# Cross-attention and feed-forward block: VectorE's low halves of weights and turned tokens at the end of its feed-forward slot, the second x1 turning two slots after the first

## The chip, the cores and the metric

The kernel runs on one core of a Trainium2 chip. Its time is the device time of one execution in microseconds (us); the figure compared is the median of several. The engines are TensorE (PE: matmuls), VectorE (DVE), ScalarE (ACT), GpSimd (POOL) and SyncE (SP: here it issues nearly all DMAs).

## The reference

Sixteen batches of 512 tokens, model width 512, 16 heads of 32, feed-forward width 2048:

```python
q, k, v = heads(x @ Wq + bq), heads(ctx @ Wk + bk), heads(ctx @ Wv + bv)
scores = einsum('bhqd,bhkd->bhqk', q, k) / sqrt(32)
attn = softmax(where(j < i, scores, -1e30)); attn[:, :, 0, :] = 0
x1 = layer_norm(x + merge(attn @ v) @ Wo + bo) * g1 + be1
out = layer_norm(x1 + relu(x1 @ W1 + b1) @ W2 + b2) * g2 + be2
```

Everything is float32. The kernel writes each float32 operand as a high half (a rounded copy) and a low half (operand minus high half) and makes a product of three matmuls: high by high, high by low, low by high.

## The kernel before, in words

Two programs, `attention` and `feed`, are each written as five generators, one per engine, which yield once per slot. `side_by_side` runs the attention's slots alone for a while; from attention slot 768 + 38 on, each engine does one feed-forward slot after every two attention slots, and when the attention's 864 slots are over, the rest of the feed-forward slots follow. So the order of each engine's queue is fixed by hand, by slot numbers; engines meet only through semaphores.

The feed-forward program works on chunks of T = 256 tokens (two halves u = 0, 1 of 128), 32 chunks, each in windows of 16 slots. A step at slot number n of a chunk falls into slot n mod 16 of the window n / 16 later; `due(window, s, SLOTS, CHUNKS, first)` says for which chunk that is now. In one slot each engine goes through its steps in the order in which they are written. Three chunks overlap.

The steps of a chunk, with their slot numbers:

- LOAD (0): SyncE loads attention rows into `o_in` in 32-token blocks (8 DMAs, L847) and then x into `x_in` (L853). It waits until the previous chunk's x1 has been turned (`x1_turned`) and its residual taken. ADD_BO (2, 3): GpSimd adds the bias to `x_in` (L1096).
- OTR (turn at 2 and 4, halves at 3 and 5): VectorE transposes the blocks into `block_turned` (L1249), a single buffer; ScalarE copies the high half (L1143), VectorE subtracts to get the low half (L1264) in `turned`. A turn waits for the low half before it (`turned_lo`).
- PROJ (5, 6): TensorE multiplies by Wo into `front` (L1355); half u waits for `turned_lo`.
- RES (6, 7): VectorE adds `x_in` and takes statistics (L1286, L1190); NORM1 (8) normalises into `x1`. SyncE then stores x1 in DRAM (L1061, slot 9) and loads it back in blocks into the same `o_in` (slots 10 and 11).
- X1_TURN: VectorE turns the x1 blocks (L1249), ScalarE copies the high half (L1131), VectorE makes the low half (L1259) in `x1_halves`; GpSimd adds b2 to x1 (L1103).
- FFN1 (16 to 31): TensorE, 12 matmuls a slot into `h_ps` (L1369). The first waits for both x1 halves.
- ScalarE's relu into `hf` (L1183), GpSimd's three mixing additions (L1109 to L1112, every other slot), ScalarE's high half (L1172, odd slots) and VectorE's low half (L1329, even slots) in `hs`: the second product is made from 7 products of mixed blocks where 8 would be plain.
- FFN2 (22 to 37): TensorE, 12 or 9 matmuls a slot into `acc` (L1385).
- RES2 - 1 (37), which is slot 5: VectorE takes `acc` out in four operations (L1299 twice, L1304 twice) once 15 of the 16 FFN2 steps are done; RES2 (38): two more (L1312, L1315). STATS2 (42), NORM2 (46, slot 14): second normalisation, whose square root is ScalarE's (L1118) and whose last two operations are L1222. STORE (47, slot 15): SyncE stores `y` (L1080).
- In the first slots of the program the 48 weight pieces are split too, about 1.5 a slot in slots 5 to 33: SyncE loads, ScalarE takes the high half (L1157, L1159), VectorE the low half (L1273, L1276), and SyncE waits for the low half (`w_lo`) before it loads the next piece into the same buffer (L1076).

VectorE's steps of one slot are written in this order: turn, low half of the turned tokens, low halves of weights, RES, NORM1, RES2 - 1, RES2, STATS2, NORM2, low half of hs. The slots in which the turns and their halves stand come from one expression:

```python
for kind, at in ((0, OTR), (1, X1_TURN)):
    for u in range(U):
        for item, _ in due(window, s, SLOTS, CHUNKS, at + (1 + 2 * u, u)[kind]):
```

With kind 1 (x1) turn and halves of u are both in slot X1_TURN + u.

## Time and profile before

| | |
|---|---|
| median of 3 runs | 2663.69 us (2663.68 to 2664.45) |
| the profiled execution's own time | 2661.86 us |
| its span, first to last instruction | 2660.0 us |
| granted TensorE clock, mean | 0.987 |
| PE busy | 2596.9 us, 98% |
| VectorE busy | 2077.8 us, 78% |
| ScalarE busy | 1525.6 us, 57% |
| GpSimd busy | 1556.8 us, 59% |

Busy time is the time in which an engine executes; what is left of the span are waits. The granted clock is a share of TensorE's full speed; 1.00 is the 2.4 GHz level. In rows of the timeline the first number is the start from the span's first instruction, the second the duration, and a bracket at the end says how long the engine had been idle before and what released it. In profile rows `x` stands for x1 or x1's DRAM tensor, `x_halves` for `x1_halves`, `W` for W1 or W2.

### The profile page before, as it was taken

To read this page: it belongs to the slowest core of one execution; us is meant where nothing else is said; L and a number is where in the kernel's file an instruction comes from. 1 tells how busy PE (TensorE), PEld (TensorE's weight loads), DVE (VectorE), ACT (ScalarE), POOL (GpSimd) and SP (SyncE) were. 2 spreads that over 40 slices of the span, in tenths; PEclk is the share of its full clock that TensorE was granted. 3 is DMA by queue.
4 is the path that set the end of the run, shared out by engine and by line. 5 is a ranking of instruction groups with operands and counts; after the bars stand their busy time and mean duration, and the time that the engine had idled before them with its cause. 6 is when DMAs were issued, how large, how long until landed. Compare 5 with 4: busy or idle time off the path is not lost.

```text
span 2660.0 us, 62128 instructions
## 1 busy us (share of the span) xinstructions
PE 2596.9 (98%) x22540; PEld 2237.7 (84%) x22540; DVE 2077.8 (78%) x5171; ACT 1525.6 (57%) x2945; POOL 1556.8 (59%) x1721
## 2 busy tenths in 40 slices
PE   7999999999999999878999999999999999999998
PEld 5888888888888888757888888888888888888887
DVE  6889888988888888788767767676767676767675
ACT  4777787787777877677343434343434344444433
POOL 3777777766666666566555545454555544454543
PEclk9999999999999999978999999999999999999999
DMA  7666655565555655556132222222222222222220
GB/s 194 156 154 157 162 152 155 153 151 149 146 141 147 152 140 141 138 135 176 42 70 50 69 52 67 54 64 57 57 64 57 64 57 64 56 65 56 64 57 25
DMA packets 439556, 273.35 MB, mean 103 GB/s; under 512 B 299648, under 2 KB 334400, under 8 KB 439248
## 3 DMA queue, kind: packets, MB, share of 16 engines
q1 hardware_dynamic: 438288, 267.79, 40.4%
q8 instruction: 178, 2.92, 0.5%
q10 hardware_dynamic: 960, 1.57, 0.3%
q14 instruction: 130, 1.06, 0.1%
HBM read 109.86 MB, written 57.67 MB: 63 GB/s over the span
## 4 chain that ended last, share of the span: by engine, by line
PE 92%; DVE 3%; SPq 1%; issue 1%; DMA 1%; POOL 1%; ACT 1%; ACTq 0%; DVEq 0%; POOLq 0%
PE h_ps L1369 25%; PE acc L1385 22%; PE lin_ps L708 13%; PE front L1355 6%; PE lin_ps L704 6%; PE max_ps L683 6%; PE st_ps L730 6%; PE o_ps L750 4%; PE o_ps L752 3%; PE st_ps L765 2%; POOL prob_lo L429 1%; DVE W L1276 1%; SPq L847 0%; ACTq L492 0%; SPq L354 0%
## 5 line engine op out<-in xcount | busy, mean ns | idle before, releaser
L429 POOL TENSOR_TENSOR prob_lo<-probs,prob_hi 128x512 f16<-128x512 f32 (+1 forms) x768 | 784.4, 1035 | 371.7 <-ACT prob_hi L508 366.9
L1369 PE MATMUL h_ps<-x_halves,W 128*128 128x256 f16 x6144 | 756.4, 273 | 2.0 <-ACT hf L1183 2.0
L1385 PE MATMUL acc<-W,hs 128*128 128x256 f16 x5376 | 669.6, 273 | 1.0 <-DVE hs L1329 1.0
L1369 PEld LDWEIGHTS h_ps<-x_halves,W 128*128 128x128 f16 x6144 | 596.5, 98 | 87.8 <-issue 16.8
L1183 ACT ACTIVATE hf<-h_ps,b1s,scale_evac 128x256 f32<-128x256 f32 x512 | 284.8, 562 | 583.5 <-PE h_ps L1369 581.6
L664 DVE CUSTOM_DVE_ANT_0 max_ps<-max_ps,mask_q 128x128 f32<-128x128 f32 (+3 forms) x1024 | 485.5, 505 | 129.3 <-PE max_ps L683 113.2
L1385 PEld LDWEIGHTS acc<-W,hs 128*128 128x128 f16 x5376 | 525.9, 98 | 62.2 <-issue 1.5
L506 ACT ACTIVATE probs<-st_ps 128x512 f32<-128x512 f32 (+1 forms) x768 | 406.5, 529 | 244.2 <-PE st_ps L765 227.2
L1109 POOL TENSOR_TENSOR hf<-hf 128x256 f32<-128x256 f32 x256 | 237.7, 928 | 500.6 <-ACT hf L1183 500.4
L508 ACT ACTIVATE prob_hi<-st_ps 128x512 f16<-128x512 f32 (+1 forms) x768 | 406.8, 530 | 0.0
L1329 DVE TENSOR_TENSOR hs<-hf,hs 128x896 f16<-128x896 f32 x256 | 279.1, 1109 | 142.9 <-ACT hs L1172 142.9
L1172 ACT ACTIVATE hs<-hf 128x896 f16<-128x896 f32 x256 | 241.8, 945 | 239.4 <-POOL hf L1112 235.8
L730 PE MATMUL st_ps<-heads 98*128 98x512 f32 (+3 forms) x1024 | 313.5, 347 | 10.2 <-ACT prob_hi L508 5.3
L683 PE MATMUL max_ps<-heads 96*128 96x128 f32 (+3 forms) x1024 | 279.6, 325 | 11.9 <-DVE maxima L664 10.0
L750 PE MATMUL o_ps<-V,prob_hi 128*128 128x97 bf16 x2560 | 246.6, 209 | 10.9 <-DVE onorm L596 8.8
L752 PE MATMUL o_ps<-V,prob_lo 128*128 128x65 bf16 x2560 | 241.2, 194 | 0.0
L683 PEld LDWEIGHTS max_ps<-heads 96*128 96x128 f32 x1024 | 184.1, 191 | 61.1 <-DVE maxima L664 20.4
L704 PE MATMUL lin_ps<-wv,ctxT 128*128 128x512 f32 x768 | 226.1, 405 | 7.2 <-DVE ctxT L521 7.2
L708 PE MATMUL lin_ps<-xT,wq 128*128 128x512 f32 x768 | 226.1, 403 | 3.9 <-DVE vf L630 3.0
L1110 POOL TENSOR_TENSOR hf<-hf 128x256 f32<-128x256 f32 x256 | 224.3, 876 | 0.0
L750 PEld LDWEIGHTS o_ps<-V,prob_hi 128*128 128x128 f16 x2560 | 212.7, 99 | 13.0 <-DVE onorm L596 10.6
L708 PE MATMUL lin_ps<-ctxT,wk 128*128 128x512 f32 x768 | 221.0, 397 | 0.0
(119 smaller groups left out, 3761.9 us busy)
## 6 DMA issues: line engine op xcount, KB each, us to landing
heads<-stage SPq DMA_DIRECT2D x756, 128.0 KB, 2.5
raw<-in_xT SPq DMA_DIRECT2D x64, 256.0 KB, 3.1
o_in<-ctx_rows SPq DMA_DIRECT2D x256, 64.0 KB, 2.5
x_in<-in_x SPq DMA_DIRECT2D x32, 512.0 KB, 4.0
x_rows<-x SPq DMA_DIRECT2D x64, 256.0 KB, 2.1
o_in<-x_rows SPq DMA_DIRECT2D x256, 64.0 KB, 2.4
out<-y SPq DMA_DIRECT2D x32, 512.0 KB, 3.1
raw<-in_cT SPq DMA_DIRECT2D x60, 256.0 KB, 3.9
```

What stands on the lines that cost most here:

```text
L429: pool.tensor_tensor(prob_lo[:, k % 4, 0:w], probs[:, k % PROBS, 0:w], prob_hi[:, k % 4, 0:w], ALU.subtract).then_inc(pl_done, 1)
L506: act.activation(probs[:, k % PROBS, 0:w], st_ps[:, k % 2, 0:w], ACT.Exp, bias=PROB_BIAS, scale=SCALE)
L508: act.activation(prob_hi[:, k % 4, 0:w], st_ps[:, k % 2, 0:w], ACT.Exp, bias=PROB_BIAS, scale=SCALE).then_inc(exp_done, 1)
L664: last = dve.tensor_tensor_reduce(out=scores[:, a, :], in0=scores[:, a, :], in1=mask, scale=1.0, scalar=MASKED, op0=ALU.add, op1=ALU.max, ...
L683: last = pe.matmul(max_ps[:, bank, a * w:(a + 1) * w], heads[0:96, t, 0, i, q * P:(q + 1) * P], heads[0:96, t, 1, i, 0:w], start=(a == 0), ...
L704: last = pe.matmul(lin_ps[:, n % 2, :], a[:, aw, j, t * P:(t + 1) * P], W[kind][:, aa, j, :], start=(j == 0 and m == 0), stop=(j == KT - 1 ...
L708: last = pe.matmul(lin_ps[:, n % 2, :], W[kind][:, aw, j, t * P:(t + 1) * P], a[:, aa, j, :], start=(j == 0 and m == 0), stop=(j == KT - 1 ...
L730: last = pe.matmul(st_ps[:, k % 2, at:at + w], heads[0:98, t, 1, i, kt * P:(kt + 1) * P], heads[0:98, t, 0, i, kt * P:S], start=(opens and ...
L750: pe.matmul(o[:, 0:3 * HD + 1], prob_hi[:, k % 4, col:col + P], v[:, 0:3 * HD + 1], start=(k % 3 == 0 and q == 0), stop=False, skip_group_ ...
L752: last = pe.matmul(o[:, HD:3 * HD + 1], prob_lo[:, k % 4, col:col + P], v[:, HD:3 * HD + 1], start=False, stop=(c == 2), skip_group_check= ...
L1369: last = pe.matmul(h_ps[:, f % 2, 0:T], W1[:, aw, j, f * P:(f + 1) * P], x1_halves[:, item.parity, aa, j, :], start=(j == 0 and m == 0), s ...
L1385: last = pe.matmul(acc_products[:, n, :], hs[:, p % HS, aa, n, :], W2[:, p, aw, n, :], start=(p == 0 and m == 0 and n % 2 == 0), stop=(p = ...
```

## The change

Three things move; no operation is added or removed.

1. VectorE's low halves of turned tokens (both kinds) and of weights stand at the end of the feed-forward slot, behind the low half of hs; the turns stay at its start.
2. X1_TURN is 12 where it was 13, and the second x1 turn is two slots behind the first: turns in slots 12 and 14 (were 13 and 14), high and low halves in slots 13 and 15 (were 13 and 14).
3. GpSimd's additions of b2 follow X1_TURN: slots 12 and 13 (were 13 and 14).

```diff
@@ -888,7 +888,7 @@
     PROJ = 5
     RES = 6
     NORM1 = 8
-    X1_TURN = 13
+    X1_TURN = 12
     FFN1 = 16
     FFN2 = FFN1 + 6
     RES2 = FFN2 + FT
@@ -1121,7 +1121,7 @@
             for s in range(SLOTS):
                 for kind, at in ((0, OTR), (1, X1_TURN)):
                     for u in range(U):
-                        for item, _ in due(window, s, SLOTS, CHUNKS, at + (1 + 2 * u, u)[kind]):
+                        for item, _ in due(window, s, SLOTS, CHUNKS, at + 1 + 2 * u):
                             n = U * kind + u
                             both = turned[:, item.parity, :, :, u * P:(u + 1) * P]
                             if kind:
@@ -1242,40 +1242,17 @@
                                       ).then_inc(bo_step, 1)
                 for kind, at in ((0, OTR), (1, X1_TURN)):
                     for u in range(U):
-                        for item, _ in due(window, s, SLOTS, CHUNKS, at + (2 * u, u)[kind]):
+                        for item, _ in due(window, s, SLOTS, CHUNKS, at + 2 * u):
                             wait_for(dve, (early.o_loaded, x1_loaded)[kind][u], 64, item, 64)
 
                             wait_for(dve, turned_lo, 2 * U, item, U * kind + u)
                             dve.transpose(block_turned[:, :, :].bitcast(U32),
                                           o_in[:, u, :].bitcast(U32).rearrange("p (k t) -> p k t", t=P)
                                           ).then_inc((ctx_turned, x1_turned)[kind], 1)
-                for kind, at in ((0, OTR), (1, X1_TURN)):
-                    for u in range(U):
-                        for item, _ in due(window, s, SLOTS, CHUNKS, at + (1 + 2 * u, u)[kind]):
-                            n = U * kind + u
-                            wait_for(dve, turned_hi, 2 * U, item, n + 1)
-                            if kind:
-                                both = x1_halves[:, item.parity, :, :, u * P:(u + 1) * P]
-                                dve.scalar_tensor_tensor(out=both[:, 1, :, :], in0=block_turned[:, :, :],
-                                                         scalar=scale_x1, in1=both[:, 0, :, :], op0=ALU.mult,
-                                                         op1=ALU.subtract).then_inc(turned_lo, 1)
-                                continue
-                            both = turned[:, item.parity, :, :, u * P:(u + 1) * P]
-                            dve.tensor_tensor(both[:, 1, :, :], block_turned[:, :, :], both[:, 0, :, :], ALU.subtract
-                                              ).then_inc(turned_lo, 1)
                 if (window, s) == (0, OTR + 1):
                     dve.wait_ge(bv_hi, 1)
                     dve.tensor_tensor(bv_parts[:, 1, :, :], bvc[:, :].unsqueeze(2).to_broadcast([P, KT, P]),
                                       bv_parts[:, 0, :, :], ALU.subtract).then_inc(bv_lo, 1)
-                for n in weights_due(window, s):
-                    dve.wait_ge(w_hi, n + 1)
-                    if n < KT:
-                        dve.tensor_tensor(part_of(n, 1), raw_slot(n), part_of(n, 0), ALU.subtract
-                                          ).then_inc(w_lo, 1)
-                    else:
-                        dve.scalar_tensor_tensor(out=part_of(n, 1), in0=raw_of(n), scalar=weight_scale[n],
-                                                 in1=part_of(n, 0), op0=ALU.mult, op1=ALU.subtract
-                                                 ).then_inc(w_lo, 1)
                 for u in range(U):
                     for item, _ in due(window, s, SLOTS, CHUNKS, RES + u):
                         wait_for(dve, proj_done, U, item, u + 1)
@@ -1328,6 +1305,29 @@
                         wait_for(dve, h_hi, PAIRS, item, p + 1)
                         dve.tensor_tensor(hs[:, p % HS, 1, :, :], hf[:, (PAIRS * item.n + p) % HF, 1:1 + PRODUCTS, :],
                                           hs[:, p % HS, 0, :, :], ALU.subtract).then_inc(h_lo, 1)
+                for kind, at in ((0, OTR), (1, X1_TURN)):
+                    for u in range(U):
+                        for item, _ in due(window, s, SLOTS, CHUNKS, at + 1 + 2 * u):
+                            n = U * kind + u
+                            wait_for(dve, turned_hi, 2 * U, item, n + 1)
+                            if kind:
+                                both = x1_halves[:, item.parity, :, :, u * P:(u + 1) * P]
+                                dve.scalar_tensor_tensor(out=both[:, 1, :, :], in0=block_turned[:, :, :],
+                                                         scalar=scale_x1, in1=both[:, 0, :, :], op0=ALU.mult,
+                                                         op1=ALU.subtract).then_inc(turned_lo, 1)
+                                continue
+                            both = turned[:, item.parity, :, :, u * P:(u + 1) * P]
+                            dve.tensor_tensor(both[:, 1, :, :], block_turned[:, :, :], both[:, 0, :, :], ALU.subtract
+                                              ).then_inc(turned_lo, 1)
+                for n in weights_due(window, s):
+                    dve.wait_ge(w_hi, n + 1)
+                    if n < KT:
+                        dve.tensor_tensor(part_of(n, 1), raw_slot(n), part_of(n, 0), ALU.subtract
+                                          ).then_inc(w_lo, 1)
+                    else:
+                        dve.scalar_tensor_tensor(out=part_of(n, 1), in0=raw_of(n), scalar=weight_scale[n],
+                                                 in1=part_of(n, 0), op0=ALU.mult, op1=ALU.subtract
+                                                 ).then_inc(w_lo, 1)
                 yield
 
     def tensor(pe):
```

How it moves instructions on VectorE, first in the second half of a chunk's window once all weights are split. hs is the low half of the mixed activations, x1_halves the x1 low half, y the NORM2 part. Before:

```order
L1249 STREAM_TRANSPOSE block_turned<-o_in 128x512
L1259 SCALAR_TENSOR_TENSOR x_halves<-block_turned,scale,x_halves 128x4x128
L1249 STREAM_TRANSPOSE block_turned<-o_in 128x512
L1259 SCALAR_TENSOR_TENSOR x_halves<-block_turned,scale,x_halves 128x4x128
L1210 RECIPROCAL rs<-sd 128x2
L1212 SCALAR_TENSOR_TENSOR rs<-rs 128x2
L1215 TENSOR_TENSOR rs<-rs,ve 128x2
L1217 SCALAR_TENSOR_TENSOR rs<-rs 128x2
L1222 SCALAR_TENSOR_TENSOR y<-y,rs,vec_be 128x512 x2
L1329 TENSOR_TENSOR hs<-hf,hs 128x896 x2
L1249 STREAM_TRANSPOSE block_turned<-o_in 128x512
```

After (line numbers of the changed file: L1306 is hs, L1315 the x1 low half):

```order
L1306 TENSOR_TENSOR hs<-hf,hs 128x896
L1315 SCALAR_TENSOR_TENSOR x_halves<-block_turned,scale,x_halves 128x4x128
L1249 STREAM_TRANSPOSE block_turned<-o_in 128x512
L1210 RECIPROCAL rs<-sd 128x2
L1212 SCALAR_TENSOR_TENSOR rs<-rs 128x2
L1215 TENSOR_TENSOR rs<-rs,ve 128x2
L1217 SCALAR_TENSOR_TENSOR rs<-rs 128x2
L1222 SCALAR_TENSOR_TENSOR y<-y,rs,vec_be 128x512 x2
L1306 TENSOR_TENSOR hs<-hf,hs 128x896
L1315 SCALAR_TENSOR_TENSOR x_halves<-block_turned,scale,x_halves 128x4x128
L1306 TENSOR_TENSOR hs<-hf,hs 128x896
L1249 STREAM_TRANSPOSE block_turned<-o_in 128x512
```

The first turn is one hs earlier, the first x1 low half stands behind the hs of slot 12, and the second x1 low half, which stood ahead of NORM2 (L1210 to L1222) and its hs, stands behind both. On ScalarE the second x1 high half is correspondingly behind NORM2's square root and one relu.

VectorE in slots 4 to 6 of a window, from the second context turn on. y<-acc is RES2 - 1, x1<-front the first residual. Before:

```order
L1249 STREAM_TRANSPOSE block_turned<-o_in 128x512
L1329 TENSOR_TENSOR hs<-hf,hs 128x896
L1264 TENSOR_TENSOR turned<-block_turned,turned 128x4x128
L1299 SCALAR_TENSOR_TENSOR y<-acc,scale_evac,x 128x512 x2
L1304 SCALAR_TENSOR_TENSOR y<-acc,scale_evac,y 128x512
L1304 SCALAR_TENSOR_TENSOR y<-acc,scale_less,y 128x2x256
L1286 TENSOR_TENSOR x<-front,x_in 128x512
```

After (L1320 is the context low half, L1276 and L1281 the four of RES2 - 1):

```order
L1249 STREAM_TRANSPOSE block_turned<-o_in 128x512
L1306 TENSOR_TENSOR hs<-hf,hs 128x896
L1276 SCALAR_TENSOR_TENSOR y<-acc,scale_evac,x 128x512 x2
L1281 SCALAR_TENSOR_TENSOR y<-acc,scale_evac,y 128x512
L1281 SCALAR_TENSOR_TENSOR y<-acc,scale_less,y 128x2x256
L1320 TENSOR_TENSOR turned<-block_turned,turned 128x4x128
L1263 TENSOR_TENSOR x<-front,x_in 128x512
```

The second context low half has moved from before the four operations of RES2 - 1 to behind them; TensorE's second projection waits for it.

VectorE in slots 14 and 15 of the first window, beside the attention's last steps (osum, onorm) and with weights still to be split. Operations of the attention's maximum, of which there are none in this piece, would have line L664. Before:

```order
L1249 STREAM_TRANSPOSE block_turned<-o_in 128x512
L1259 SCALAR_TENSOR_TENSOR x_halves<-block_turned,scale,x_halves 128x4x128
L1276 SCALAR_TENSOR_TENSOR W<-raw,scale,W 128x512
L585 TENSOR_REDUCE osum<-o_ps 128x128
L588 RECIPROCAL o_ps<-o_ps 128x4
L596 TENSOR_TENSOR onorm<-osum,o_ps 128x4x32
L1276 SCALAR_TENSOR_TENSOR W<-raw,scale,W 128x512 x2
```

After (L1328 is the weights' low half):

```order
L1249 STREAM_TRANSPOSE block_turned<-o_in 128x512
L1328 SCALAR_TENSOR_TENSOR W<-raw,scale,W 128x512
L585 TENSOR_REDUCE osum<-o_ps 128x128
L588 RECIPROCAL o_ps<-o_ps 128x4
L596 TENSOR_TENSOR onorm<-osum,o_ps 128x4x32
L1315 SCALAR_TENSOR_TENSOR x_halves<-block_turned,scale,x_halves 128x4x128
L1328 SCALAR_TENSOR_TENSOR W<-raw,scale,W 128x512 x2
```

The second x1 low half has moved from before one weight low half and one set of osum and onorm to behind them. In the slots that follow, the weights' low halves likewise stand behind the slot's hs and residual where they stood ahead.

## Rows read from the trace of the kernel before

**Rows 1.** Busy time by stretch (us): engines, granted clock (PEclk), DMA share, GB/s

```profile
1160.00:1200.00 40.00, 25.64 (x197) 19.80 (x196) 36.01 (x73) 29.54 (x58) 24.15 (x22) 0.68 0.43 114
1200.00:1260.00 60.00, 51.65 (x430) 42.97 (x431) 50.56 (x73) 42.60 (x73) 36.95 (x36) 0.90 0.64 175
1260.00:2640.00 1380.00, 1380.00 (x11838) 1213.51 (x11836) 971.00 (x1590) 566.73 (x924) 697.71 (x863) 1.00 0.25 58
```

**Rows 2.** TensorE's waits, 1110 to 1330 us: in total, times, longest

```profile
PE o_ps L750 <- DVE onorm L596: 8.8, 3, 4.7
...
PE front L1355 <- DVE turned L1264: 2.8, 2, 2.2
PE h_ps L1369 <- ACT hf L1183: 2.0, 3, 1.2
...
PE acc L1385 <- DVE hs L1329: 1.0, 1, 1.0
```

**Rows 3.** Timeline (start us, us, ...), VectorE, slots 12 to 15, one chunk

```profile
1876.27 0.71 DVE L1249 STREAM_TRANSPOSE block_turned<-o_in 128x512 uint32<-128x512 uint32 x1 [2.00 <-DMA o_in<-x_rows]
...
1880.56 0.92 DVE L1259 SCALAR_TENSOR_TENSOR x_halves<-block_turned,scale,x_halves 128x512 f16<-128x512 f32 x1 [0.79 <-ACT x_halves L1131]
...
1882.18 1.41 DVE L1222 SCALAR_TENSOR_TENSOR y<-y,rs,vec_be 128x512 f32<-128x512 f32 x2
```

**Rows 4.** Timeline, ScalarE, same chunk, slots 13 and 14

```profile
1878.48 0.55 ACT L1183 ACTIVATE hf<-h_ps,b1s,scale_evac 128x256 f32<-128x256 f32 x1
...
1880.56 0.56 ACT L1183 ACTIVATE hf<-h_ps,b1s,scale_evac 128x256 f32<-128x256 f32 x1
```

**Rows 5.** Timeline, TensorE, next item's slots 0, 4 and 6

```profile
1883.96 1.47 PE L1369 MATMUL h_ps<-x_halves,W 128*128 128x256 f16 x12
...
1895.10 1.47 PE L1385 MATMUL acc<-W,hs 128*128 128x256 f16 x12
...
1901.39 3.02 PE L1355 MATMUL front<-Wo,turned 128*128 128x512 f32 x12
```

**Rows 6.** Timeline, VectorE, slots 4 and 5 of that item

```profile
1898.25 1.19 DVE L1329 TENSOR_TENSOR hs<-hf,hs 128x896 f16<-128x896 f32 x1 [4.87 <-ACT hs L1172]
1899.68 0.89 DVE L1264 TENSOR_TENSOR turned<-block_turned,turned 128x512 fp32r<-128x512 f32 x1 [0.24 <-ACT turned L1143]
1900.50 1.40 DVE L1299 SCALAR_TENSOR_TENSOR y<-acc,scale_evac,x 128x512 f32<-128x512 f32 x2
...
1902.60 0.74 DVE L1304 SCALAR_TENSOR_TENSOR y<-acc,scale_less,y 128x512 f32<-128x512 f32 x1
```

**Rows 7.** Timeline, GpSimd, slot 2: the bias addition

```profile
1894.19 1.26 POOL L1096 TENSOR_TENSOR x_in<-x_in,bo_row 128x512 f32<-128x512 f32 x1 [7.06 <-DMA x_in<-in_x]
```

**Rows 8.** Timeline, SyncE's queue: the store of y

```profile
1883.62 0.39 SPq L1080 DMA_DIRECT2D out<-y  x1
```

**Rows 9.** Timeline, VectorE and TensorE, slots 4 and 6, a looser chunk

```profile
2480.10 1.18 DVE L1329 TENSOR_TENSOR hs<-hf,hs 128x896 f16<-128x896 f32 x1 [4.00 <-ACT hs L1172]
...
2484.48 2.79 PE L1355 MATMUL front<-Wo,turned 128*128 128x512 f32 x11
```

**Rows 10.** Timeline, VectorE, transition: slots 13, 14, 20 and 21

```profile
1195.09 0.68 DVE L1249 STREAM_TRANSPOSE block_turned<-o_in 128x512 uint32<-128x512 uint32 x1
...
1199.79 0.70 DVE L1249 STREAM_TRANSPOSE block_turned<-o_in 128x512 uint32<-128x512 uint32 x1
...
1203.02 1.64 DVE L1276 SCALAR_TENSOR_TENSOR W<-raw,scale,W 128x512 f16<-128x512 f32 x1
...
1222.99 0.75 DVE L1276 SCALAR_TENSOR_TENSOR W<-raw,scale,W 128x512 f16<-128x512 f32 x1 [1.64 <-ACT W L1159]
...
1225.20 0.94 DVE L1264 TENSOR_TENSOR turned<-block_turned,turned 128x512 fp32r<-128x512 f32 x1
```

**Rows 11.** Timeline, SyncE's queue, transition: x1 and next context blocks

```profile
1189.35 2.90 SPq L847 DMA_DIRECT2D o_in<-x_rows  x4
...
1205.18 6.26 SPq L847 DMA_DIRECT2D o_in<-ctx_rows  x8
```

## What I expect of it

> **What bounds the kernel now.** The page comes first: TensorE is busy 98% of the span, VectorE 78%. The busy time by stretch then says where the other 2% lie [rows 1]. From 1260 to 2640 us, the part in which only the feed-forward program runs, TensorE is busy in 1380.00 of 1380.00 us at full granted clock (1.00, the 2.4 GHz level). Nothing that VectorE gains there can shorten it; a new wait can only lengthen it. Between 1160 and 1200 us TensorE idles 14.36 us and between 1200 and 1260 us 8.35 us, at granted clocks of 0.68 and 0.90. There the attention program runs out while the feed-forward program starts, with every weight still to be split, and VectorE is busy in 36.0 of 40 and 50.6 of 60 us. So there are two questions: what of the 8.35 us comes back, and does the full stretch stay full?
>
> The waits of TensorE over the transition [rows 2] name the releasers: VectorE's onorm (8.8 us in 3 waits), its turned (2.8 us), ScalarE's hf (2.0 us), VectorE's hs (1.0 us).
>
> **The change, part by part.** Nothing is removed or added: the same low halves (0.7 to 1.8 us each in the rows), ScalarE copies and additions of b2, elsewhere in their queues. TensorE's and SyncE's queues keep their order.
>
> *1. The steady chunk, slots 12 to 15.* In the chunk of [rows 3] VectorE turns the x1 tokens at 1876.27, after 2.00 us of waiting for the load, waits for ScalarE's high half, makes the low, turns again, waits again (0.79 us in the row), and ends the second low at 1880.56 + 0.92 = 1881.48. Only then come NORM2's small operations and its final pair, which ends at 1882.18 + 1.41 = 1883.59, 2.11 us behind the low. In the new order the second low is in slot 15, behind NORM2 and behind slot 14's hs. NORM2 then hangs on ScalarE, whose root is in slot 14 behind the relu that ends at 1878.48 + 0.55 = 1879.03 [rows 4]. I take NORM2's end at 1879.03 + 2.11 + 0.2 for the root = 1881.3: 2.3 us earlier.
>
> *2. The x1 low.* TensorE's first feed-forward product of the next item starts at 1883.96 [rows 5] and needs the second x1 low. Behind NORM2 (1881.3) and one hs (1.19 in rows 6) it starts at about 1882.5. ScalarE's half is there by then: its relu at 1880.56 ends at 1881.12 [rows 4], plus 0.79 (the wait for such a copy) is 1881.9. The low ends at 1882.5 + 0.92 = 1883.4. Before, it was ready 2.48 us ahead of the need; now about 0.5 us ahead. No wait, but little left.
>
> *3. The second context low, slot 5.* This is the place that decides. Before, it stands ahead of the four operations that empty acc: hs 1898.25 to 1899.44, low 1899.68 to 1900.57, then the four from 1900.50 to 1902.60 + 0.74 = 1903.34 [rows 6]. TensorE's second projection takes the low at 1901.39 [rows 5]. Now it stands behind the four, which take 2.84 us. If hs came no earlier, the low would end at 1899.44 + 2.84 + 0.89 = 1903.17, and TensorE would wait 1.78 us in each chunk. But hs does come earlier. It is late because GpSimd's bias addition waits 7.06 us for x_in until 1894.19 [rows 7]; x_in is loaded behind the store of y and the o_in blocks on SyncE's queue, and that store is issued at 1883.62, right behind NORM2's end [rows 8]. With NORM2 2.3 us earlier the whole chain is 2.3 us earlier: hs from 1895.95 to 1897.14. The four need TensorE's slot-4 product, done at 1895.10 + 1.47 = 1896.57 [rows 5], so that does not hold them. The low ends at 1897.14 + 2.84 + 0.89 = 1900.87, 0.52 us before its need. This is the tightest chunk I read, with hs 3.14 us ahead of the projection; in a looser one it is 2484.48 - 2480.10 = 4.38 us ahead [rows 9]. **Steady chunks cost nothing, at margins of about 0.5 us at two places**; I add 0.5 us in all for a few that miss. Bounds: 0, and 1.78 us in each of some 29 chunks, 52 us.
>
> One thing works against even the 0.52 us. The same kind of operation on 128x512 takes 0.92 us in one place and 1.64 us in another [rows 3, 10], a spread of 0.72 us. If the low of slot 5 met the long form in each tight chunk, TensorE would wait 0.72 - 0.52 = 0.2 us there, under 6 us over all 29, and the sum would be near +2; I keep that as a bound. The Trainium skill (SBUF — State Buffer, "SBUF: two separate sides") says that a VectorE operation with two SBUF inputs and a GpSimd operation that reads SBUF lock each other out of a shared port pair for a whole instruction, and GpSimd's mixing is now beside the low. By that rule the long form is the one to expect, and no row here shows who holds whom.
>
> *4. The transition, chunk 0.* VectorE's slot 14 was turn at 1199.79, a wait, the low at 1201.28 (1.81 us long), the weight low at 1203.02 (to 1204.66), and only then the attention's osum and onorm [rows 10]. The low goes to slot 15, and its wait goes. From the turn's end, 1200.49, to the weight low's start are 2.53 us; the weight low and onorm come forward by at most that, and by less where ScalarE's own half of the weight or a store ahead in SyncE's queue holds. I take 1.5 us, bounds 0 and 2.5. One of the three waits for onorm is behind it. SyncE issues the loads of chunk 1 at 1205.18, directly behind that weight low [rows 11], so x_in, the mixing and the second projection of chunk 1 are earlier by about 1.5 us, too.
>
> *5. Chunk 1, slots 20 and 21.* Before, the weight low at 1222.99, which had waited 1.64 us for ScalarE, stands ahead of hs and of the turned low at 1225.20, whose end at 1226.14 releases the projection. With hs ahead of the weight low VectorE works during that wait. Gain about 1 us. Parts 4 and 5 together bring the projection 2.5 us earlier; the bounds are 0 and the 2.8 us of turned plus the 2.0 of hf.
>
> *6. Behind it.* The hs wait (1.0 us) was for a half that stood behind normalisation and a weight low; it goes, and part of the 2.0 us on hf with it: I take 1.5 us, bounds 0 and 3.0.
>
> *7. The early turn, chunk 0.* Turning in slot 12 instead of 13 puts VectorE in front of a load. It turned at 1195.09 without a wait for it; the blocks are issued from 1189.35 to 1192.25 [rows 11], and the steady turn waited up to 2.00 us. With a landing near 1194 and slot 12 reached near 1193, VectorE stands about 1 us, with the attention's osum and the weight low of that slot behind it. The attention's output tile is double, so most is hidden: no cost I take, bounds -0.5 and +2.
>
> *8. b2 in slots 12 and 13.* GpSimd's first b2 addition now stands ahead of one mixing; GpSimd's idle time, 7.06 us before one operation of the chunk [rows 7], hides it. If the cover were gone, it would cost one addition, 1.26 us there. The tail behind the last product holds none of the moved operations: 0.
>
> Sum: +0.5 - 2.5 - 1.5 = **-3.5 us**. On the profiled execution's 2661.86 that is 2658.4. The runs' median is 1.83 us above that execution, so on the median 2663.69 - 3.5 = **2660.2 us**. This kernel's measurement tells about 0.2%, 5.3 us, from no change; the forecast is within it.
>
> **Rivals.**
> - *A new wait at the second projection of every chunk.* The place is slot 5, part 3. It decides from the point where hs starts less than 1.19 + 2.84 + 0.89 = 4.92 us ahead of the projection; at 3.14 before, it needs 1.8 of the 2.3 us that NORM2 gives. For it: the whole margin is 0.5 us and rests on a DMA chain of 10.6 us (1883.62 to 1894.19). Against it: the looser chunks need only 0.5 us, and the chain has no other gate in the rows. If half of the advance arrives, TensorE waits 0.6 us in the tight half of 29 chunks, some +9 us, less 3.5 of the transition: 2669. If none, up to 1.78 x 29 less 3.5, 2712; in looser chunks 0.54 us each, 2676. I give all of it 0.14.
> - *More comes back.* All 8.35 us of 1200 to 1260 and nothing new: 2655.3. For it: onorm, turned, hs and hf all wait behind weight lows; an earlier end of the low clock (0.68 and 0.90 in rows 1) could add to it. Against it: VectorE stays busy in 50.6 of 60 us, and its work is the same. 0.28.
> - *Nothing arrives.* The transition is bound by the sum of VectorE's work, and an early stall in slot 12 eats what the reordering frees: 2663.7, between 2661.7 and 2666. 0.20.
> - The forecast, gain between 1.5 and 5.3 us: 0.38.
>
> **How the numbers follow.** Faster by over 0.2% (below 2658.4) is the second rival and little of the forecast: 0.28. Slower by over 0.2% (above 2669.0) is most of the first, 0.12, the rest of which lands within: same 0.60. The range begins at 2655.5, since nothing in rows 1 offers more than 8.35 us; it ends at 2668.5, which takes in the empty case and the mild form of the first rival and leaves out about 1 in 10 above.
>
> **What would show it.** TensorE still full from 1260 on, with no wait for turned in steady chunks; NORM2 ending some 2.3 us earlier against TensorE, and hs of slot 4 likewise; the low of slot 5 behind the four, just ahead of the projection; a second projection of chunk 1 nearer 1223.5 than 1226.2; fewer waits for turned, hs and hf. Wrong, if TensorE shows a short wait before each second projection, or if an onorm wait grows behind the turn in slot 12.

## The result, and the profile after

The changed kernel takes 2669.3 us (median of 20 runs, 2665.67 to 2672.4), the kernel before 2664.14 us (20 runs, 2658.62 to 2667.5). The ratio is 1.0019, 95% interval 1.0013 to 1.0025: some 5 us slower, where I forecast 3.5 us less, and outside my range of 2655.5 to 2668.5.

Busy time by stretch, changed kernel (us: the stretch, then TensorE's matmuls, its weight loads, VectorE, ScalarE, GpSimd; then granted clock, DMA share, GB/s). The first two lines answer to the last two of [rows 1], the third begins where the first chunks are through:

```profile
1200.00:1260.00 60.00, 51.10 (x425) 42.50 (x426) 55.49 (x76) 44.62 (x77) 40.32 (x36) 0.90 0.65 180
1260.00:2640.00 1380.00, 1378.49 (x11794) 1207.42 (x11792) 1020.94 (x1583) 562.56 (x920) 683.02 (x860) 1.00 0.25 58
1320.00:2640.00 1320.00, 1318.49 (x11288) 1155.05 (x11287) 976.89 (x1517) 537.79 (x879) 650.91 (x821) 1.00 0.25 58
```

The stretch that was full is not quite full any more: 1318.49 of 1320.00 us. That is less than the loss: waits of a few tenths hardly show in the matmuls' busy time (their ends are modelled). They do show ahead of the weight loads, changed kernel, 1320 to 2640 us (in total, times, longest):

```profile
PEld front L1355 <- DVE turned L1320: 4.5, 11, 1.1
```

Before, there is no such wait in the stretch. The start of the second projection of each chunk is the better clock. TensorE, changed kernel, one early chunk and two later ones (x6, x11 and, further down, x8 stand where the view's window ends: each projection has twelve matmuls):

```profile
1319.18 3.06 PE L1355 MATMUL front<-Wo,turned 128*128 128x512 f32 x12
...
1815.62 1.66 PE L1355 MATMUL front<-Wo,turned 128*128 128x512 f32 x6 [0.78 <-DVE turned L1320]
...
2041.53 2.79 PE L1355 MATMUL front<-Wo,turned 128*128 128x512 f32 x11
```

And before, the same projections of the first and the last of these chunks:

```profile
1318.29 3.02 PE L1355 MATMUL front<-Wo,turned 128*128 128x512 f32 x12
...
2035.95 3.02 PE L1355 MATMUL front<-Wo,turned 128*128 128x512 f32 x12
```

Sixteen chunks took 2035.95 - 1318.29 = 717.66 us before (44.85 each) and 2041.53 - 1319.18 = 722.35 us now: **4.69 us lost here**, 0.29 a chunk. From the first projection of a chunk to the second were 5.06 us before; now eleven of the sixteen take longer, which makes 4.07 of the 4.69 us, and most of the rest stands between chunks, at two waits of weight loads for the x1 low (0.6 us). The last twelve chunks of the stretch lose nothing (538.23 before, 538.25 now). The transition gives nothing to set against it: the second projection of chunk 1 starts at 1226.35, before at 1226.19.

VectorE in slots 13 to 5 of the chunk that answers to [rows 3, 6], changed kernel (L1315 x1 low, L1306 hs low, L1276 and L1281 the four of RES2 - 1, L1320 context low):

```profile
1881.25 1.66 DVE L1315 SCALAR_TENSOR_TENSOR x_halves<-block_turned,scale,x_halves 128x512 f16<-128x512 f32 x1 [1.12 <-ACT x_halves L1131]
...
1883.65 0.12 DVE L1210 RECIPROCAL rs<-sd 128x2 f32<-128x2 f32 x1
1883.81 0.24 DVE L1212 SCALAR_TENSOR_TENSOR rs<-rs 128x2 f32<-128x2 f32 x1
1884.09 0.65 DVE L1215 TENSOR_TENSOR rs<-rs,ve 128x2 f32<-128x2 f32 x1
1884.77 0.38 DVE L1217 SCALAR_TENSOR_TENSOR rs<-rs 128x2 f32<-128x2 f32 x1
1885.18 1.42 DVE L1222 SCALAR_TENSOR_TENSOR y<-y,rs,vec_be 128x512 f32<-128x512 f32 x2
1886.51 1.09 DVE L1306 TENSOR_TENSOR hs<-hf,hs 128x896 f16<-128x896 f32 x1
1887.52 0.75 DVE L1315 SCALAR_TENSOR_TENSOR x_halves<-block_turned,scale,x_halves 128x512 f16<-128x512 f32 x1
...
1901.55 1.17 DVE L1306 TENSOR_TENSOR hs<-hf,hs 128x896 f16<-128x896 f32 x1 [3.77 <-ACT hs L1172]
1902.64 1.40 DVE L1276 SCALAR_TENSOR_TENSOR y<-acc,scale_evac,x 128x512 f32<-128x512 f32 x2
1904.07 0.75 DVE L1281 SCALAR_TENSOR_TENSOR y<-acc,scale_evac,y 128x512 f32<-128x512 f32 x1
1904.73 0.74 DVE L1281 SCALAR_TENSOR_TENSOR y<-acc,scale_less,y 128x512 f32<-128x512 f32 x1
1905.39 0.68 DVE L1320 TENSOR_TENSOR turned<-block_turned,turned 128x512 fp32r<-128x512 f32 x1
```

TensorE of that chunk (first feed-forward product, first and second projection), which answers to [rows 5]:

```profile
1888.36 1.47 PE L1369 MATMUL h_ps<-x_halves,W 128*128 128x256 f16 x12
...
1900.72 2.99 PE L1355 MATMUL front<-Wo,turned 128*128 128x512 f32 x12
...
1906.13 2.11 PE L1355 MATMUL front<-Wo,turned 128*128 128x512 f32 x8
```

The context low ends at 1905.39 + 0.68 = 1906.07 and the projection starts 0.06 us later. Between the two projections lie 5.41 us; in chunks that wait for nothing it is 5.06, so 0.35 us are a wait. The needed lead of hs is 1906.13 - 1901.55 = 4.58 us (4.59 in most chunks that wait), not the 4.92 that I had by adding durations, since each operation starts up to 0.1 us before the one ahead is recorded as ended. And the x1 low of slot 15 ends at 1887.52 + 0.75 = 1888.27, 0.09 us before the product at 1888.36: on the edge, too.

GpSimd and SyncE of the same chunk, which answer to [rows 7, 8]:

```profile
1897.48 1.27 POOL L1096 TENSOR_TENSOR x_in<-x_in,bo_row 128x512 f32<-128x512 f32 x1 [6.53 <-DMA x_in<-in_x]
```

```profile
1886.63 0.40 SPq L1080 DMA_DIRECT2D out<-y  x1
```

Against the undisturbed schedule (the projection less its wait, 1905.78) the store of y is issued 19.15 us ahead. In the chunk of [rows 8] it was 1901.39 - 1883.62 = 17.77 us, but that chunk was not typical. Of the 29 chunks from 1318.29 on, 23 had their store 18.46 or 18.47 us ahead of the projection before, as here (the second projection of this chunk starts at 1408.00):

```profile
1386.76 0.16 DVE L1210 RECIPROCAL rs<-sd 128x2 f32<-128x2 f32 x1
1386.95 0.49 DVE L1212 SCALAR_TENSOR_TENSOR rs<-rs 128x2 f32<-128x2 f32 x1
1387.48 0.38 DVE L1215 TENSOR_TENSOR rs<-rs,ve 128x2 f32<-128x2 f32 x1
1387.89 0.16 DVE L1217 SCALAR_TENSOR_TENSOR rs<-rs 128x2 f32<-128x2 f32 x1
1388.09 1.42 DVE L1222 SCALAR_TENSOR_TENSOR y<-y,rs,vec_be 128x512 f32<-128x512 f32 x2
```

That is the kernel before, one typical NORM2: 2.75 us from the reciprocal's start to the end of y, where the chunk that I read had 2.19. Now it takes 2.95. It starts 0.88 us earlier against the schedule and lasts 0.2 longer, so **the store comes 0.69 us earlier, not 2.3**.

**In total that is about the loss.** At the sixteen projections that end these chunks (1363.15 to 2035.95 before), hs of slot 4 started 3.14 to 4.36 us ahead in the kernel before. Add 0.69 to each, subtract from the 4.59 that are needed, and keep what is positive: thirteen are short, by 4.3 us together; measured were 4.07 at these projections. At the twelve projections behind them the lead before was 4.10 to 4.45, with 0.69 always over 4.59: nothing lost, as measured. But the count does not say which chunk waits: of the thirteen, nine waited; four, three of them counted 0.48 to 0.68 us short, did not, and two that were counted safe waited 0.35 and 0.25 us. So the size of the sum is in part luck.

Why the leads differ stands in SyncE's queue. Kernel before, the blocks and x of a chunk with a lead of 3.22 us (projection at 1587.41), and the blocks of one with 4.23 (2349.92):

```profile
1569.51 6.47 SPq L847 DMA_DIRECT2D o_in<-ctx_rows  x8
1576.02 0.63 SPq L853 DMA_DIRECT2D x_in<-in_x  x1
...
2332.02 5.44 SPq L847 DMA_DIRECT2D o_in<-ctx_rows  x8
```

Issuing the eight block loads puts x_in 6.06 to 7.07 us behind the store of y in the sixteen chunks (mean 6.5) and 6.04 to 6.27 in the twelve (mean 6.1); from the issue of x_in to hs are 7.8 to 8.6 us in all. So the early chunks are the tight ones because SyncE takes longer over the same loads there, and the lead of a given chunk differs from one trace to the next. Why it takes longer was not tried.

### The profile page after: what moved, and what is told of

It reads as the page before. It is cut to its first block, busy times and chain, and to the rows that moved or that the text cites. A ratio compares the mean times of both kernels' runs of the same rounds, so it can differ in the third digit from the quotient of the medians.

```text
span 2665.6 us, 62128 instructions
## 1 busy us (share of the span) xinstructions
PE 2600.8 (98%) x22540; PEld 2236.9 (84%) x22540; DVE 2133.9 (80%) x5171; ACT 1524.0 (57%) x2945; POOL 1546.9 (58%) x1721
## 4 chain that ended last, share of the span: by engine, by line
PE 84%; DVE 5%; SPq 3%; issue 2%; DMA 2%; POOL 2%; ACT 1%; ACTq 0%; DVEq 0%; POOLq 0%
PE h_ps L1369 21%; PE acc L1385 18%; PE lin_ps L708 13%; PE lin_ps L704 6%; PE max_ps L683 6%; PE st_ps L730 6%; PE front L1355 5%; PE o_ps L750 4%; PE o_ps L752 3%; SPq L847 2%; PE st_ps L765 2%; DMA x_in<-in_x 1%; DVE W L1328 1%; POOL prob_lo L429 1%; DVE x_halves L1315 1%
## 5 line engine op out<-in xcount | busy, mean ns | idle before, releaser
L664 DVE CUSTOM_DVE_ANT_0 max_ps<-max_ps,mask_q 128x128 f32<-128x128 f32 (+3 forms) x1024 | 486.3, 506 | 130.6 <-PE max_ps L683 114.2
L1109 POOL TENSOR_TENSOR hf<-hf 128x256 f32<-128x256 f32 x256 | 234.8, 917 | 531.7 <-ACT hf L1183 531.7
L1306 DVE TENSOR_TENSOR hs<-hf,hs 128x896 f16<-128x896 f32 x256 | 281.5, 1100 | 124.9 <-ACT hs L1172 124.8
L1110 POOL TENSOR_TENSOR hf<-hf 128x256 f32<-128x256 f32 x256 | 211.6, 827 | 0.0
```

The costliest lines, as they stand in the source:

```text
L664: last = dve.tensor_tensor_reduce(out=scores[:, a, :], in0=scores[:, a, :], in1=mask, scale=1.0, scalar=MASKED, op0=ALU.add, op1=ALU.max, ...
```

## The experiments

**Theory A**: the second projection waits because the context low stands behind the four operations, and the x1 part gives too little lead to make up for it. **Rival B**: more work on VectorE beside GpSimd (its busy time from 1320 to 2640 us rose from 927.19 to 976.89 us) delays everything a little. **Rival C**: the weights' low halves in the transition.

### Undo one part, do one part

In the diffs `...` stands for lines left out. `e1_ctx_mid`, the changed kernel with the context low halves back in the middle of the slot, ahead of RES, and without kind 0 at the end:

```diff
+                for u in range(U):
+                    for item, _ in due(window, s, SLOTS, CHUNKS, OTR + 1 + 2 * u):
+                        wait_for(dve, turned_hi, 2 * U, item, u + 1)
...
-                for kind, at in ((0, OTR), (1, X1_TURN)):
+                for kind, at in ((1, X1_TURN),):
```

> The changed kernel with one part undone: the context tokens' low halves stand in the middle of VectorE's slot again, ahead of the four operations that empty acc; the x1 and weight halves stay at the end. If the steady part's loss comes from the second context low standing behind those four (theory A), the projections stand 44.85 us apart again from 1320 us on and about 4.7 us come back: near 2664.5 on the median, 0.0 to +1.0 over the kernel before. If the loss comes from VectorE and GpSimd getting in each other's way in the new slots 12 to 15 (theory B), most of it stays: 2668 to 2669.

`e2_ctx_end`: the kernel before, with the context low halves alone moved to the slot's end.

```diff
-                for kind, at in ((0, OTR), (1, X1_TURN)):
+                for kind, at in ((1, X1_TURN),):
...
                                           hs[:, p % HS, 0, :, :], ALU.subtract).then_inc(h_lo, 1)
+                for u in range(U):
+                    for item, _ in due(window, s, SLOTS, CHUNKS, OTR + 1 + 2 * u):
```

> The kernel before with that part alone: the context lows at the end of the slot, everything else as before. Theory A: the hs of slot 4 starts 3.1 to 4.4 us ahead of the second projection and would need 4.6 us, so each steady chunk waits 0.2 to 1.4 us: +10 to +25 us over the kernel before, more than the whole change, since the earlier normalisation does not help here. Theory B: no loss beyond 1 us.

`e3_weights_end`: the kernel before, with the whole `weights_due` loop, of which the diff shows the first lines, alone moved to the slot's end.

```diff
-                for n in weights_due(window, s):
-                    dve.wait_ge(w_hi, n + 1)
...
                                           hs[:, p % HS, 0, :, :], ALU.subtract).then_inc(h_lo, 1)
+                for n in weights_due(window, s):
+                    dve.wait_ge(w_hi, n + 1)
```

> The kernel before with the weights' lows alone at the end of the slot. It can act only up to about 1262 us. The forecast's parts 5 and 6 gave it a gain of 2 to 3 us; the trace of the changed kernel, whose second projection of chunk 1 starts 0.2 us later and that of chunk 2 0.8 us later than before, speaks for nothing: within 1.5 us of the kernel before.

`e4_x_first`: the changed kernel with the load of x ahead of the blocks.

```diff
+        sp.dma_start(self.x_in[:, :, :], x.rearrange("(u p) n -> p u n", p=P)).then_inc(self.x_loaded, 16)
         for u in range(self.U):
             self.load_blocks(sp, u, ctx_rows[u * P:(u + 1) * P, :], self.o_loaded)
-        sp.dma_start(self.x_in[:, :, :], x.rearrange("(u p) n -> p u n", p=P)).then_inc(self.x_loaded, 16)
```

> The changed kernel, with SyncE's load of x_in ahead of the eight blocks of o_in rather than behind them. Theory A in its full form, that the slot-4 hs is late through the chain store of y, o_in blocks, x_in, bias addition, mixing: the bias addition starts some 5 us earlier, hs over 6 us ahead of the second projection, no wait in any steady chunk, and the transition, too, has x_in earlier: -5 to -8 us against the changed kernel, 2661 to 2664. If hs does not come earlier, another gate stands behind x_in: about 2669.

Measured, beside 27 runs of the kernel before with a median of 2664.0 us:

| run | median, us (runs) | ratio to before, 95% interval | PE busy, 1320 to 2640 us |
|---|---|---|---|
| e1_ctx_mid | 2663.89 (11) | 1.0001, 0.9992 to 1.0010 | 1320.00 |
| e2_ctx_end | 2683.57 (5) | 1.0069, 1.0057 to 1.0082 | 1309.06 |
| e3_weights_end | 2663.56 (11) | 0.9997, 0.9989 to 1.0006 | 1320.00 |
| e4_x_first | 2663.41 (11) | 0.9996, 0.9987 to 1.0004 | 1320.00 |

TensorE's waits in e2 from 1110 to 2640 us (engine, tile, line; in total, times, longest):

```profile
PE front L1361 <- DVE turned L1335: 15.7, 20, 3.5
```

Putting the context low back (e1) takes the whole loss away. Its trace also shows the leads of the new order where nothing waits for them: the store is 19.15 us ahead, and the sixteen leads are 3.86 to 4.97 us, on average 0.70 more than before. Eleven of them are under 4.59, by 4.3 us together; the changed kernel had eleven waits and 4.07 us. The other twelve are 4.72 to 5.22, none short. Moving the context low alone (e2) costs 19.6 us; by the same count on the leads of before, now without the 0.69 us, 29 chunks should lose 19.2. So the x1 part does help by some 0.7 us a chunk, and it isn't enough. Loading x first reaches the same end from the other side: hs starts 6.63 to 8.45 us ahead of the projection in the 28 chunks from 1340 us on, far over 4.59, with the low half still behind the four. In e1 VectorE is busy 990.16 us of the stretch, more than in the changed kernel, and the second projections wait for nothing: rival B falls. e3 shows no price of the weights' move: rival C falls. All four runs came out as theory A expected.

### The x1 part, and b2

`e5_x1_part`: the kernel before, with turns in slots 12 and 14, x1 low halves in 13 and 15 at the slot's end, b2 in 12 and 13; context and weight low halves stay in the middle.

```diff
-    X1_TURN = 13
+    X1_TURN = 12
...
-                        for item, _ in due(window, s, SLOTS, CHUNKS, at + (2 * u, u)[kind]):
+                        for item, _ in due(window, s, SLOTS, CHUNKS, at + 2 * u):
...
                                           hs[:, p % HS, 0, :, :], ALU.subtract).then_inc(h_lo, 1)
+                for kind, at in ((1, X1_TURN),):
+                    for u in range(U):
+                        for item, _ in due(window, s, SLOTS, CHUNKS, at + 1 + 2 * u):
```

> The kernel before with the x1 part alone: turns in slots 12 and 14, halves in 13 and 15 with the lows at the slot's end, b2 in slots 12 and 13; context and weight lows in the middle. Expected: y's store 19.15 us ahead of the second projection (18.46 before), steady chunks full, and one new wait of about 1.9 us for the second x1 low at chunk 1's first feed-forward product. On the median 0 to +2 over the kernel before. The rival, that what VectorE loses to GpSimd's b2 costs TensorE time in steady chunks, says +3 to +5.

`e6_b2_late`, the changed kernel with b2 where it was:

```diff
-                    for item, _ in due(window, s, SLOTS, CHUNKS, X1_TURN + u):
+                    for item, _ in due(window, s, SLOTS, CHUNKS, X1_TURN + 1 + u):
```

> The changed kernel with GpSimd's b2 additions back in slots 13 and 14. If they are what makes VectorE's second-normalisation products long (mean 1390 ns against 825 before), that mean falls back below 900 ns and VectorE's busy time from 1320 to 2640 us from 977 to about 935. The time stays near 2669, because y's store hangs on ScalarE's root, which does not move; the rival, that this long product delays the slot-4 chain, says 2665 to 2667.

`e7_before_x_first` and `e8_weights_end_x_first`: the kernel before with the load of x first (the diff of e4), without and with the weights' low halves at the slot's end.

> The kernel before with x_in loaded ahead of the o_in blocks and nothing else. In steady chunks the hs of slot 4 comes 3 to 4 us earlier, which buys nothing, TensorE being full. In the transition chunk 1's mixing no longer waits for x_in: the waits for turned (2.8 us) and hf (2.0 us) may shrink: -1 to -3 us. If VectorE's sum of work is what binds the transition, 0.

> The kernel before with the weights' lows at the end of the slot and x_in loaded first, context and x1 lows as before: the two parts that showed no new wait, together. The stretch from the first projection of chunk 0 to the second of chunk 1 was 66.3 us before and 64.0 with the weights' lows at the end: -2 to -4 us on the median if both gains reach the end, 0 if they are the same gain or if the stretch's start moves against them.

Beside 27 runs of the kernel before with a median of 2664.15 us:

| run | median, us (runs) | ratio to before, 95% interval | PE busy, 1320 to 2640 us |
|---|---|---|---|
| e5_x1_part | 2669.82 (11) | 1.0017, 1.0008 to 1.0026 | 1320.00 |
| e6_b2_late | 2682.86 (5) | 1.0061, 1.0048 to 1.0074 | 1313.79 |
| e7_before_x_first | 2662.25 (11) | 0.9990, 0.9981 to 0.9999 | 1320.00 |
| e8_weights_end_x_first | 2662.19 (11) | 0.9995, 0.9986 to 1.0004 | 1320.00 |

e5 missed my expectation of 0 to +2 us. Its steady stretch is full, with the store 19.15 us ahead as expected, so the rival of a loss in steady chunks does not hold either. What is new are two waits in the transition, where I had expected one of 1.9 us, TensorE:

```profile
1210.75 2.65 PE L1375 MATMUL h_ps<-x_halves,W 128*128 128x256 f16 x12 [2.81 <-DVE x_halves L1330]
```

```profile
1260.79 1.55 PE L1375 MATMUL h_ps<-x_halves,W 128*128 128x256 f16 x12 [2.89 <-DVE x_halves L1330]
```

They make 5.7 us, and the median is 5.7 us up; but the other waits of the transition moved too (onorm 11.4 us where it was 8.8, others less), so that the two agree is no proof. Ahead of the second, on VectorE, stand the slot's two weight low halves (L1268), which in the changed kernel stand behind the x1 low (L1330):

```profile
1258.67 1.40 DVE L1268 SCALAR_TENSOR_TENSOR W<-raw,scale,W 128x512 f16<-128x512 f32 x2
1259.99 0.74 DVE L1330 SCALAR_TENSOR_TENSOR x_halves<-block_turned,scale,x_halves 128x512 f16<-128x512 f32 x1
```

e6 missed its expectation by more. I had made b2 the reason for longer VectorE operations: y's scaling (L1202) has a mean of 827 ns before and 1373 ns in the changed kernel. That did fall back, to 884 ns, but VectorE's busy time stayed at 977.46 us, and the kernel became 11 us slower than the changed one (by their ratios 1.0061 and 1.0019). TensorE's waits, 1110 to 2640 us, e6:

```profile
PE h_ps L1369 <- DVE x_halves L1315: 8.2, 26, 3.4
```

and VectorE, then GpSimd, of one chunk there:

```profile
1891.51 0.65 DVE L1217 SCALAR_TENSOR_TENSOR rs<-rs 128x2 f32<-128x2 f32 x1
1892.19 1.57 DVE L1222 SCALAR_TENSOR_TENSOR y<-y,rs,vec_be 128x512 f32<-128x512 f32 x2
...
1894.69 0.74 DVE L1315 SCALAR_TENSOR_TENSOR x_halves<-block_turned,scale,x_halves 128x512 f16<-128x512 f32 x1
```

```profile
1887.83 2.94 POOL L1103 TENSOR_TENSOR x<-x,vec_b 128x512 f32<-128x512 f32 x2
1890.73 0.72 POOL L1109 TENSOR_TENSOR hf<-hf 128x256 f32<-128x256 f32 x1
1891.41 0.73 POOL L1110 TENSOR_TENSOR hf<-hf 128x256 f32<-128x256 f32 x1
```

Both b2 additions now run together, and the mixing behind them lies beside NORM2's small operations and the start of its last pair. NORM2 takes 1890.38 to 1893.76, 3.38 us instead of 2.95. The hs and the x1 low behind it are later by that, and the 0.09 us of margin are gone: the low ends at 1895.43, and TensorE, which starts the product at 1895.49, had been waiting for 0.21 us. Over the stretch the weight loads of that product wait 13.0 us for the x1 low, where they waited 0.6 in the changed kernel. So the b2 slots belong to the x1 part: part 8, which I costed at nothing, guards the second tight place.

e7 came as expected, some 1.9 us under the kernel before. e8 did not: at 2662.19 us it is no better than e7, so the weights' move adds nothing to the load order.

### Two last questions

`e9_x1_slots_only`: the kernel before, with the slots of e5, but every low half in the middle, the x1 low ahead of the slot's weights.

```diff
-    X1_TURN = 13
+    X1_TURN = 12
...
-                        for item, _ in due(window, s, SLOTS, CHUNKS, at + (1 + 2 * u, u)[kind]):
+                        for item, _ in due(window, s, SLOTS, CHUNKS, at + 1 + 2 * u):
...
-                        for item, _ in due(window, s, SLOTS, CHUNKS, at + (2 * u, u)[kind]):
+                        for item, _ in due(window, s, SLOTS, CHUNKS, at + 2 * u):
...
-                        for item, _ in due(window, s, SLOTS, CHUNKS, at + (1 + 2 * u, u)[kind]):
+                        for item, _ in due(window, s, SLOTS, CHUNKS, at + 1 + 2 * u):
```

> The kernel before with the x1 part moved (turns in slots 12 and 14, low halves in 13 and 15, b2 in 12 and 13), but every low half left in the middle of its slot, and the x1 low half ahead of its slot's W low halves. Theory A (in the run with the x1 part alone and everything else at the end, the 2.81 and 2.89 us waits of the first product in the first two chunks came from the weight low halves of slot 15 standing ahead of the x1 low half, 1.5 to 1.7 us each): the two waits fall to 1 to 1.5 us, and the median is 0 to 2 us over the kernel before. Theory B (turning the second half two slots later is late by itself, whatever stands ahead of its low half): the waits stay at 2.8 us, and the median is again 5 us or more over the kernel before.

`e10_low_halfway`, the changed kernel with the second context low between the first two and the last two of the four operations. The function that the diff calls, not shown, makes the low half; it is called again at the slot's end, for slots without these operations:

```diff
                                                  in1=x1[:, item.parity, u, :], op0=ALU.mult, op1=ALU.add
                                                  ).then_inc(y_part, 1)
+                    second_context_low(waiting)
                     wait_for(dve, y_part, 6, item, 2)
```

> The changed kernel with the second context low half neither in the middle of the slot nor at its end: it stands behind the second of the four additions, ahead of the third and fourth. Theory A (the second projection waits because hs, the four additions and the context low half need 4.6 us one after the other, and many chunks have less): two additions of some 0.7 us fewer stand ahead, the needed lead falls to about 3.2 us, less than any chunk showed (3.86 us or more with the low half in the middle), the waits from 1320 us on are gone and the median is 2662 to 2665 us. Theory B (only the old place in the middle avoids it, since the following work is then in the way of something else): the median stays at 2668 us or more.

Beside 21 runs of the kernel before with a median of 2664.45 us: e9 2667.2 us (11 runs, ratio 1.0008, 0.9999 to 1.0016), e10 2665.06 us (11 runs, 1.0001, 0.9992 to 1.0010). The stretch from 1320 us on is full in both.

In e9 the waits for x_halves shrink from 5.7 (e5) to 2.5 us in total, about what theory A of that run said and what the changed kernel has (2.4):

```profile
PE h_ps L1369 <- DVE x_halves L1259: 2.5, 2, 1.6
```

The excess over the kernel before goes from 5.7 to 2.8 us, a little over the 2 us that I allowed; its interval reaches from nothing to 4 us. VectorE in e10:

```profile
1903.04 1.18 DVE L1316 TENSOR_TENSOR hs<-hf,hs 128x896 f16<-128x896 f32 x1 [3.87 <-ACT hs L1172]
1904.14 1.40 DVE L1285 SCALAR_TENSOR_TENSOR y<-acc,scale_evac,x 128x512 f32<-128x512 f32 x2
1905.46 0.68 DVE L1232 TENSOR_TENSOR turned<-block_turned,turned 128x512 fp32r<-128x512 f32 x1
```

The low ends at 1906.14, the projection starts at 1907.18: with hs 4.14 us ahead, which would have been 0.45 us short in the changed kernel, 1.04 us are to spare. Over the sixteen chunks the leads are 4.06 to 5.00 us there, eleven under 4.59, and none waits. It is the operations ahead of the low that make the wait; moving it ahead of two of the four is enough.

## Why the prediction was wrong

The step that failed is in part 1: "I take NORM2's end at 1879.03 + 2.11 + 0.2 for the root = 1881.3: 2.3 us earlier." The start was right: NORM2 hangs on ScalarE's root behind the relu I named and begins 22.13 us ahead of the projection, where I had 1901.39 - 1879.19 = 22.20. The length was wrong, 2.95 us for 2.11, and the starting point was wrong: I measured the gain from the one chunk with the latest store of y (17.77 us ahead, 18.46 in most). In that chunk the store came 1.4 us earlier, in most 0.69. And a low needed behind the four operations was tested against one lead, where the leads of sixteen chunks differ by over 1 us with SyncE's time for the block loads, which the prediction took as fixed.

- *Part 2, the x1 low*: margin forecast 0.5 us, measured 0.09. In the changed kernel's steady chunks nearly no wait (0.6 us in two, of TensorE's weight loads), but e6 shows how thin it is.
- *Part 3, the context low*: the mechanism was right, and so was the place. The needed lead is 4.59 us where I had 4.92; the lead given was 0.69 us more and not 2.3. It was part 3's "0.52 us before its need" that fell, and with it the cost of 0.5: measured 4.69, of which 4.07 at these projections.
- The long form of the low, my bound of part 3, didn't come: its mean is 687 ns now and 794 ns before. What part 3 had wrong there is who stands beside the low. In the chunk at 1905.39 GpSimd ended its mixing at 1903.97 + 0.45 = 1904.42 and begins again only 0.54 us into the low (0.68 us long), while before it mixed from 1898.75 to 1901.58 beside a low of 0.89 us:

```profile
1905.93 0.74 POOL L1109 TENSOR_TENSOR hf<-hf 128x256 f32<-128x256 f32 x1 [1.51 <-ACT hf L1183]
```

  The rule of the Trainium skill (SBUF — State Buffer, "SBUF: two separate sides") by which I would have expected the long form is about two operations that overlap, so it is not tested there; it fits what happened to NORM2, below.
- *Parts 4 to 6, the transition*: -4 us forecast. From the first projection of chunk 0 to the second of chunk 1 were 1226.19 - 1159.91 = 66.28 us and are 1226.35 - 1161.61 = 64.74, 1.5 us less where I had 2.5. But this is one execution of each, and the moment at which the stretch begins moves by itself, 1160 to 1166 us over the profiled executions. Behind it, to the second projection of chunk 3, 92.10 us have become 92.83. The hs wait of 1.0 us is gone, as forecast, the waits for turned went from 2.8 to 2.4 and those for hf from 2.0 to 1.6, and a wait of the kind that I left out has come, TensorE, changed kernel:

```profile
1207.75 2.74 PE L1369 MATMUL h_ps<-x_halves,W 128*128 128x256 f16 x12 [0.44 <-DVE x_halves L1315]
...
1256.79 1.48 PE L1369 MATMUL h_ps<-x_halves,W 128*128 128x256 f16 x12 [1.94 <-DVE x_halves L1315]
```

  Part 2 should have been worked out for chunks 0 and 1 as well, where weight low halves share VectorE's slots. e1, with the same order there but for the context low in the middle, stands at 1.0001 of the kernel before: the transition is worth nothing in sum.
- *Part 7, the early turn*: about 1 us forecast, 1.30 measured (VectorE, changed kernel), and no wait for onorm grew behind it (9.0 us in 4, before 8.8 in 3):

```profile
1195.47 0.71 DVE L1249 STREAM_TRANSPOSE block_turned<-o_in 128x512 uint32<-128x512 uint32 x1 [1.30 <-DMA o_in<-x_rows]
```

- *Part 8, b2*: nothing forecast, and nothing lost by it; but my reason (GpSimd's idle time hides it) looked at GpSimd alone.

The rival that happened is the first, in its mild form: "some +9 us, less 3.5 of the transition: 2669." It names 2669 and the median is 2669.3, though by luck: the waits were half of that and the transition gave nothing. I gave it 0.14 and ended the range at 2668.5, because I held a margin of 0.5 us on one chunk for a margin in all.

No version beats both kernels by a margin that stands. The lowest ratio is that of the kernel before with x loaded first (e7), which is no part of the change: 0.9990, interval 0.9981 to 0.9999, some 1.9 us, under the 5 us that I called measurable.

## What to carry to other kernels

Where an order by hand moves an operation behind others on an engine, write down the lead that it now needs and compare it with the lead in every repetition, not in one: the leads of 3.14 to 4.45 us over the 29 chunks stood in the trace of before. With the needed 4.59 and the gain of 0.69, both measured only afterwards, the sum of the shortages comes within 0.3 us of the waits at these projections, though not chunk by chunk. A gain that is to pay for such a move has to be read against the same clock (TensorE's schedule), and its own operations' durations from the typical repetition. What moves on a third engine (here GpSimd's b2) can be part of the margin even when that engine has time.

## What I had not expected of the hardware

The same VectorE operation takes longer or shorter by what GpSimd does beside it. In the changed kernel the x1 low takes 1.66 us at 1881.25, beside a b2 addition, and 0.75 us at 1887.52, in a gap of GpSimd's. GpSimd, changed kernel:

```profile
1881.09 1.27 POOL L1103 TENSOR_TENSOR x<-x,vec_b 128x512 f32<-128x512 f32 x1
1883.31 0.73 POOL L1109 TENSOR_TENSOR hf<-hf 128x256 f32<-128x256 f32 x1 [0.94 <-ACT hf L1183]
1883.99 0.73 POOL L1110 TENSOR_TENSOR hf<-hf 128x256 f32<-128x256 f32 x1
```

It reaches operations on two numbers a partition: L1215 took 0.65 us at 1884.09, just until GpSimd's addition from 1883.99 ended (1884.72 against 1884.74), and L1217 is 0.16 us long in the typical chunk of before, where GpSimd was idle, and 0.38 here, until GpSimd's last mixing addition ended (1884.67 + 0.46 = 1885.13 against 1885.15). The reciprocal ahead of them, with one input, is as short here (0.12 us at 1883.65, in the middle of a GpSimd addition) as anywhere (0.16 in the chunk of before). Who waits for whom has shifted, too: over the whole span VectorE's busy time went from 2077.8 to 2133.9 us, while GpSimd's fell from 1556.8 to 1546.9, with the same operations on both. The Trainium skill (SBUF — State Buffer, "SBUF: two separate sides") says that when a VectorE operation with two SBUF inputs meets a GpSimd operation that reads SBUF, whichever starts first holds the shared port pair for its whole instruction and the other fully blocks. The trace agrees, in that the 0.65 and the 0.38 us end with GpSimd's instructions; the 1.66 us are 0.91 more than 0.75, less than the 1.11 us for which the addition was still running, so there it agrees only roughly. It costs time only where a margin is smaller than the blocked stretch.
